# A decoder layer on one core: fp16 pairs, transposes by DMA, and a longer software pipeline

## What is computed

```
x = x + attention(layernorm(x))      # 8 heads of 128; q and k are RMS-normalised, turned (rotary),
                                     # causal softmax, products with wo
x = x + gelu(layernorm(x) @ ctx.T) @ ctx          # ctx: 375 rows of 256, one set per batch
x = x + ffn(layernorm(x))            # 256 -> 1024 -> 256, inputs, weights and biases
                                     # rounded to fixed point and clipped, relu between
```

## Time and profile before

| | |
|---|---|
| median of 3 runs | 731.43 us (731.16 to 732.57) |
| the profiled execution | 730.79 us |
| its span, first to last instruction | 729.1 us |
| PE, PEld busy | 697.2 us (96%), 609.9 us (84%) |
| DVE, ACT, POOL busy | 642.4 us (88%), 486.9 us (67%), 248.3 us (34%) |
| TensorE's granted clock, mean | 0.986 |
| DMA | 38.86 MB, 53 GB/s over the span |

### The profile page before, as it was taken

How to read it: one execution, slowest core, us unless ns; L and a number is a source line. 1 busy time by engine, 2 the same in 40 slices (tenths; PEclk the granted TensorE clock), 3 DMA queues, 4 the chain that set the end, 5 groups by cost and what they waited for, 6 DMA issues and landing times.

```text
span 729.1 us, 15114 instructions
## 1 busy us (share of the span) xinstructions
PE 697.2 (96%) x5504; PEld 609.9 (84%) x5504; DVE 642.4 (88%) x1232; ACT 486.9 (67%) x1226; POOL 248.3 (34%) x393
## 2 busy tenths in 40 slices
PE   5599999999999999999999999999999999999974
PEld 4488888888888888888888989889888888888863
DVE  6989999999999999999999999999999999998942
ACT  5667766677766677776667767666777766677742
POOL 1344333433332343333234243333334333433310
PEclk9899999999999999999999999999999999999996
DMA  8501110111111011111111111101111110111100
GB/s 268 204 8 49 49 48 24 54 57 49 55 48 42 26 55 55 48 52 51 32 35 55 55 48 48 52 22 47 55 53 50 48 47 24 54 50 43 49 7 13
DMA packets 23946, 38.86 MB, mean 53 GB/s; under 512 B 2048, under 2 KB 18896, under 8 KB 23664
## 3 DMA queue, kind: packets, MB, share of 16 engines
q1 hardware_dynamic: 23920, 38.51, 17.5%
HBM read 34.84 MB, written 3.67 MB: 53 GB/s over the span
## 4 chain that ended last, share of the span: by engine, by line
PE 89%; DVE 3%; ACT 3%; issue 2%; DMA 2%; SPq 0%; POOL 0%; POOLq 0%; DVEq 0%; ACTq 0%
PE psum L846 34%; PE psum L833 17%; PE psum L874 7%; PE psum L854 6%; PE psum L911 6%; PE psum L920 6%; PE psum L945 4%; PE psum L937 3%; PE psum L881 3%; PE psum L902 2%; DMA w_raw<-in_wv 1%; DMA w_raw<-in_w 1%; ACT qkn L743 1%; PE psum L927 1%; DVE turn_c L492 0%
## 5 line engine op out<-in xcount | busy, mean ns | idle before, releaser
L846 PE MATMUL psum<-wqkv_hi,xnT_hi 128*112 128x512 f32 x384 | 165.1, 430 | 4.8 <-DVE wqkv_lo L433 2.8
L846 PE MATMUL psum<-wqkv_lo,xnT_hi 128*112 128x512 f32 x384 | 152.3, 397 | 0.0
L846 PE MATMUL psum<-wqkv_hi,xnT_lo 128*112 128x512 f32 x384 | 131.4, 396 | 0.0
L697 ACT ACTIVATE sq<-psum 112x1024 f32<-112x1024 f32 x64 | 65.5, 1023 | 79.7 <-PE psum L846 79.7
L344 POOL TENSOR_TENSOR rstd<-ve,nhalf 112x1 f32<-112x1 f32 x96 | 55.4, 578 | 156.0 <-DVE ve L407 151.0
L351 POOL TENSOR_TENSOR rms<-ms,nhalf 112x8 f32<-112x8 f32 x64 | 106.3, 1662 | 5.0
L733 ACT ACTIVATE w_raw<-psum,rden 112x128 f32<-112x128 f32 x256 | 69.5, 384 | 45.7 <-DVE rden L519 45.7
L846 PEld LDWEIGHTS psum<-wqkv_hi,xnT_lo 128*112 128x112 f32 x384 | 67.5, 176 | 22.1
L846 PEld LDWEIGHTS psum<-wqkv_hi,xnT_hi 128*112 128x112 f32 x384 | 68.1, 177 | 21.4 <-issue 3.1
L476 DVE TENSOR_TENSOR turn_c<-psum,cos_t 112x1024 f32<-112x1024 f32 x64 | 78.1, 1220 | 6.2 <-ACT sq L697 5.6
L468 DVE TENSOR_REDUCE ss<-sq 112x4 f32<-112x512 f32 (+1 forms) x95 | 81.9, 862 | 0.0
(11 more groups left out here) (82 smaller groups left out, 1531.4 us busy)
## 6 DMA issues: line engine op xcount, KB each, us to landing
ctx_in<-in_ctx_rows SPq DMA_DIRECT2D x32, 375.0 KB
ctxT<-in_ctx_cols SPq DMA_DIRECT2D x32, 375.0 KB, 6.4
x_in<-in_x SPq DMA_DIRECT2D x32, 112.0 KB, 2.0
out_y<-y_out SPq DMA_DIRECT2D x32, 112.0 KB, 1.9
w_raw<-in_w SPq DMA_DIRECT2D x2, 1024.0 KB, 7.5
w_raw<-in_wq SPq DMA_DIRECT2D x2, 512.0 KB, 4.6
w_raw<-in_wk SPq DMA_DIRECT2D x2, 512.0 KB, 6.3
w_raw<-in_wv SPq DMA_DIRECT2D x2, 512.0 KB, 8.0
```

The source lines that it names most:

```text
L846: last = pe.matmul(ps[:, n, :], left[:, c, :], right[:, c, w, n * BANK:(n + 1) * BANK], start=c == 0 and left is xnT_hi and right is wqkv_ ...
```

## The change

It does eight things.

1. The weights wq, wk, wv, wo become fp16 pairs. Each is first scaled by a power of two: ScalarE squares it and sums along rows, TensorE sums over the partitions with a matrix of ones, VectorE bounds the sum, GpSimd takes the inverse root, VectorE keeps its exponent bits (`lift_weights`). The scales are taken back in the RMS constant for q and k, and in `residual_attention`, now a `scalar_tensor_tensor` with y_unit. Projections come in the order k, q, v.
2. xn and o become fp16 pairs, made before the transpose: ScalarE rounds (`round_xn`, `round_o`), VectorE subtracts (`split_xn`, `split_o`). So do q (`round_q0`, `round_q1` on ScalarE by head; `split_q` on VectorE by head, eight `scalar_tensor_tensor`) and k (`scale_k1`, `scale_k0` on ScalarE by head into kn, `round_k0`, `split_k`).
3. All 16-bit transposes, xn, q, k, o (both parts at once) and xq, are `dma_start_transpose` from SP's queue, SBUF to SBUF. Only xn2 (fp32) is still transposed on TensorE.
4. The keys' sum of cosine and sine part (`turn_k`) goes from VectorE to GpSimd.
5. `normalise_k` on VectorE is gone (see 2).
6. The PSUM banks are given out anew: q 3 and 4, k and scores 0 and 1, y 0, v 6 and 7, o 3 to 5, the FFN's hidden halves 5 and 6, ctx_out 7, and xn2T, h and the FFN's output 2.
7. p and o have buffers of their own; v's column of ones holds 16.
8. The loop is gone: 40 bodies are written out, each over up to nine batches a = i + 3 to i - 5, and the orders of all engines are new, with the waits that they need.

The core of the diff, new side first where a function is replaced as a whole:

```diff
+            def transpose_k(j):
+                sp.wait_ge(k_lo_done, done(j))
+                sp.dma_start_transpose(qkT[:, 1], qk16[:, 1].rearrange("t l n -> t (l n)")).then_inc(kT_landed, 16)
...
+            def transpose_x(j):
+                sp.wait_ge(xn_lo_done, done(j))
+                if j.has(1):
+                    sp.wait_ge(v1_ready, done(j.plus(-1)))
+                sp.dma_start_transpose(xT16[:, :, :], xn16[:, :, :].rearrange("t l n -> t (l n)")).then_inc(xT_landed, 16)
...
+            def turn_k(j):
+                pool.wait_ge(k_sin_done, done(j))
+                pool.tensor_tensor(turn_c[:, 1, :], turn_c[:, 1, :], turn_s[:, 1, :], ALU.add).then_inc(k_turned, 1)
...
+            def split_q(j):
+                dve.wait_ge(q_hi1_done, done(j))
+                for h in range(H):
+                    at = slice(h * D, (h + 1) * D)
+                    last = dve.scalar_tensor_tensor(out=qk16[:, 0, 1, at], in0=turn_c[:, 0, at], scalar=rms[:, 0, h:h + 1],
+                                                    in1=qk16[:, 0, 0, at], op0=ALU.mult, op1=ALU.subtract)
+                last.then_inc(q_lo_done, 1)
...
-                dve.tensor_tensor(heads(qkn[:, 1, :]), heads(turn_c[:, 1, :]),
-                                  rms[:, 1, :].unsqueeze(2).broadcast_to([T, H, D]), ALU.mult).then_inc(k_normed, 1)
...
+            def project_q(j):
+                if j.has(2):
+                    pe.wait_ge(o0_normed, done(j.plus(-2)))
+                if j.off == 1:
+                    pe.wait_ge(q_sin_done, done(j.plus(-1)))
+                project(0, 0, q_ps[:, 0, :], j)
+                project(0, 1, q_ps[:, 1, :], j).then_inc(q_ready, 1)
...
+                    hi, lo = xT16[:, c, :], xT16[:, MC + c, :]
+                    pe.matmul(dst, hi, wqkv[:, 0, c, w, cols], start=c == 0, stop=False)
+                    pe.matmul(dst, hi, wqkv[:, 1, c, w, cols], start=False, stop=False)
+                    last = pe.matmul(dst, lo, wqkv[:, 0, c, w, cols], start=False, stop=c == MC - 1)
```

More of the change, by code:

```diff
@@ L273, in x_at @@
[L273 to L281 removed]
+            sp.dma_start(x_in[:, 0, :], x[0:1].rearrange("o t m -> (o t) m")).then_inc(x_landed[0], 16)
@@ L321, in _ @@
+            for i in range(-3, B + 5):
+                body(i)
             for s in range(SLOTS):
@@ new lines, in round_projection, with prepare_projections @@
+            def round_projection(n):
+                for c in range(MC):
+                    act.wait_ge(w_lift_done, TURN.index(n) + 1)
+                    act.activation(wqkv[:, 0, c, n, :], w_raw[:, c, n, :], ACT.Copy, scale=w_lift[:, n:n + 1]).then_inc(w_hi_done, 1)
+            def prepare_projections():
+                one, two, three = TURN[0:3]
+                square_projection(one)
+                square_projection(two)
+                round_projection(one)
+                square_projection(three)
+                round_projection(two)
+                round_projection(three)
@@ new lines, in relu0 @@
+            def relu0(j):
+                if j.off >= B - 2:
+                    act.wait_ge(f0_ready, done(j))
+                if is_first(j):
+                    act.wait_ge(b_done, 2)
+                for c in range(0 * FC // 2, 1 * FC // 2):
+                    last = act.activation(f_int[:, c * T:(c + 1) * T], f0_ps[:, (c % (FC // 2)) * T:(c % (FC // 2) + 1) * T],
+                                          ACT.Relu, bias=b1_col[:, c:c + 1], scale=1.0 / W_FRAC)
+                last.then_inc(f0_int_done, 1)
@@ L897, in i_first, with sum_weights @@
-            def i_first(j):
-                return isinstance(j.base, int) and j.base + j.off == 0
-            def transpose_rows(dst, src, ready):
+            def sum_weights(n):
+                turn = TURN.index(n)
+                if turn == 0:
+                    pe.wait_ge(const_done, 6)
+                else:
+                    pe.wait_ge(w_sq_done, turn)
+                pe.wait_ge(w_squared, (turn + 1) * MC)
+                for c in range(MC):
+                    last = pe.matmul(w_sum_ps[:, n:n + 1], ones_pp[:, :], w_sum[:, n, c:c + 1], start=c == 0, stop=c == MC - 1)
+                last.then_inc(w_summed, 1)
@@ new lines, in project_out @@
+            def project_out(heads, j, first, last):
+                if is_first(j):
+                    pe.wait_ge(wo_done, 2)
+                for h in heads:
+                    pe.matmul(y_ps, oT16[:, h, :], wo16[:, 0, h, :], start=first and h == heads[0], stop=False)
+                    pe.matmul(y_ps, oT16[:, h, :], wo16[:, 1, h, :], start=False, stop=False)
+                    product = pe.matmul(y_ps, oT16[:, H + h, :], wo16[:, 0, h, :], start=False, stop=last and h == heads[-1])
+                return product
@@ new lines, in hidden_units0 @@
+            def hidden_units0(j):
+                if j.off == 28:
+                    pe.wait_ge(o0_normed, done(j.plus(3)))
+                if is_first(j):
+                    pe.wait_ge(w_q_done, 2)
+                for c in range(0 * FC // 2, 1 * FC // 2):
+                    for m in range(MC):
+                        last = pe.matmul(f0_ps[:, (c % (FC // 2)) * T:(c % (FC // 2) + 1) * T], w1T[:, m, c, :], xqT[:, m, :],
+                                         start=m == 0, stop=m == MC - 1)
+                last.then_inc(f0_ready, 1)
```

1267 lines of the change are left out of this document (633 added, 634 removed).

## The result

The changed kernel takes **654.65 us**, median of 4 runs (653.0 to 656.18), against 731.42 of the kernel before on the same chip: ratio 0.8947, 95% interval [0.8924, 0.8971]. The forecast was 657.0 (632 to 725). The profiled execution took 654.7 us, its span is 652.9 us, the mean granted clock 0.974.

The account below looks back on a forecast made before the run. TensorE bounded the kernel before, VectorE 9% behind; afterwards VectorE by a little, with an 18.5 us period. Fill 128 + 477 to the last keys + drain 48 + 2.8 = 656 span, time 657 us (632 to 725).

Parts of the forecast that it names:

- TensorE, 17.8 us: TensorE's work per batch: 21.4 less 2.4 for transposes moved off and 1.2 for fp16 pairs.
- VectorE, 18.1 us: VectorE's work per batch: 19.6 less 5.95 removed plus 4.5 added, making it the longest by a little.
- ScalarE, 16.8 us, and GpSimd, 10.5: Work per batch on these two engines: ScalarE 15.0 + 1.8, GpSimd 7.8 + 2.7; neither bounds.
- Stalls, 0.4 us: Waiting added per batch because TensorE and VectorE both need their whole period.
- slack of "about 1 us" at normalise_o: Room for normalise_o, between weigh_values and project_q two batches on, against 3.5 us of TensorE work.
- GpSimd, "I take 0": VectorE's slowdown beside GpSimd's keys' sum, taken as 0 as ordered; up to 1.8 us a batch kept for a rival.
- Rival B: GpSimd's sum slows VectorE, or normalise_o is late for project_q: period 20.3 us, 704 to 725 us; chance 0.22.
- DMA, 8.0 us a batch and 2.4 each: DMA engine time for all transposing transfers per batch, and for each of q, k or o; covered by their places.
- Rival C: Transposing DMAs bound: 18.8 + 3.7 = 22.5 us a batch, 761 to some 775 us; chance 0.17.
- The loop written out, 0: Instruction fetches for the written-out loop cost nothing, covered as long as they run ahead.
- TensorE's first wait on a DMA: Sign that would show the forecast wrong at once, as would a period above 20 us.
- Fill and drain, 128 and 48 us: Ends of the run: first output at about 128 us, not 74.3; last batch alone through the rest 48 us.

Follow-up runs that it names:

- e2: Changed kernel without the low fp16 parts of q for heads 4 to 7 (less VectorE work), in every batch but the first: 653.78 us.
- e9: Kernel before with only the pairs of wq, wk, wv and xn made fp16 (unscaled) in place of fp32r, transposes still on TensorE: 715.89 us.
- e3: Changed kernel without v's product of xn's low part with the weights' high part (less TensorE work), in every batch but the first: 654.17 us.
- e12: Changed kernel with two VectorE neighbours exchanged: xn's subtract and multiply ahead of the turn of q by the cosine: 691.30 us.
- e5: Changed kernel with k's 16-bit pair transposed by DMA once more per batch, into a tile nobody reads: 682.47 us.
- e14: Changed kernel with split_o later in VectorE's order and the second batch's xn made earlier, between wo's scale and split: 680.54 us.
- e6: Changed kernel with three more DMA transpositions of k's pair per batch, into spare tiles: 869.34 us.

## Why the prediction was right, step by step

- **TensorE, 17.8 us:** right in sum; e2, in which it alone is full, has 17.92. The 512-column product was put at 0.213 and is 0.216. The gain from the type was 0.9 of the 1.2 us for the projections; e9 shows 0.54, which is 36 x (0.231 - 0.216): the 0.2375 that I read for fp32r was drawn out by its late first product, the others are 0.23 apart (391.87, 392.10, 392.33). The rest of what TensorE lost, 3.47 - 0.54 = 2.9 us, is 0.2 more than the 2.7 that I gave it, so two errors in part cancel.
- **VectorE, 18.1 us:** right in sum, 17.9 by e3; "the longest by a little" was not to be told from TensorE. split_q was mis-sized: eight take 2.07 us (347.71 to 349.78), not 1.5, so 0.26 apart, not 0.19. Something else in the sum was 0.7 us too dear: 0.2 of it are the statistics (1.10 us in two places for 0.90 in one, where I added 0.4), the rest I did not trace. That the sum fits is in part luck.
- **ScalarE, 16.8 us, and GpSimd, 10.5:** 16.2 and 11.1 (90.46% and 61.88% of 17.94), hidden as forecast.
- **Stalls, 0.4 us:** there are next to none in the middle (TensorE waits 0.3 us in 100). The slack of "about 1 us" at normalise_o was right in place, wrong in kind: what is tight is the ring from turn_q over normalise_o to split_o, with 0.3 to 0.4 us. Together these put the period at 18.5 for 17.94, worth 14.6 us over 26 batches.
- **GpSimd, "I take 0":** right here, but for half of the named reason: the sum ends at 356.93, under reads of PSUM and a reduction, and the first instruction that it would hold starts at 356.98. But the price behind it was wrong. I read the earlier trace rows as 0.45 us per 0.72 of GpSimd for two SBUF operands; it is a hold until GpSimd is over (in the earlier trace rows add_b2 is over at 720.46 and quantise_x3 at 720.60), and a subtract and multiply of a single tile is held too (quantise_x3 is one). What kept the neighbours free was PSUM and the reduction, not "a single tile". e12 pays 1.35 us a batch for one exchange of neighbours. Rival B's mechanism exists; the order of this kernel steps past it by 0.05 us, which I had not worked out: that is luck.
- **DMA, 8.0 us a batch and 2.4 each:** (63.6% of 652.9 - 17.5% of 729.1) / 32 = 9.0, and 2.56. Rival C's 18.8 fell. The rooms were counted right (q: 7 us, measured 6.25), the tenants were not: SP's 2 us per issue was left out, though each queue that a step is moved to counts. e5 shows that there was no room for one issue more.
- **The loop written out, 0:** the instruction queues moved 0.84 MB in 0.5% of the span, and between 300 and 400 us the list of waits has none without a releaser. No kernel with the loop kept was run.
- **A sign that misled:** "TensorE's first wait on a DMA" was to show the forecast wrong at once. TensorE's longest wait is on one, 9.07 us for xn of the second batch at 37.91, but in the fill, and e14 shows it off the path; between 300 and 400 us it waits once for a transposition, 0.3 us.
- **Fill and drain, 128 and 48 us:** 135.4 and 52.4. 5 us of the first lie at one place: wo's scale, rounding and split were to end at 24.6, and the first turn started at 29.65, as split_wo alone waited 2.1 us for ScalarE. The early batches come 16.9 us apart (67.76, 84.69 in the chain), not 13.9 and 15.7. What makes the drain 4.4 us longer was not taken apart. This 12 us eats most of the 14.6 that the period gave: the total, 654.65 for 657, is by luck nearer to the forecast than its terms are.

## To carry to other kernels

When two engines are full, take work from both or leave it: here one alone gave nothing, and both together only as far as the next ring of waits allowed; add up that ring before trusting the second gain. Before work goes to GpSimd, list what VectorE runs beside it, and what waits for that: one plain SBUF-to-SBUF operation under a 2.4 us sum stood for the rest of the sum, and as it lay in a ring of waits in the kernel before, the same edit cost 47 us there and was worth 34 in the changed one. A DMA queue is an engine with an order of its own: price a transposition by the issuer's time and by the landing, not by the share of the DMA engines.

## What the runs showed of the hardware

- A VectorE instruction of 256 columns from one SBUF tile to another lasted 1.2 and 1.9 us beside a GpSimd sum, in place of 0.40, and was over 0.14 us behind it; a reduction and reads of PSUM did not stand. Beside GpSimd's root of eight columns the same kind of instruction took 0.41.
- A transposing transfer of 112 x 2048 fp16 between SBUF tiles: some 1.3 to 3.1 us to issue on SP, 4.0 to 6.5 us to landing, 1824 packets, 2.56 us of the 16 DMA engines.
- In e6, in which TensorE waits 4.7 us a batch at scores, the granted clock is 0.89 between 300 and 400 us, where the changed kernel has 1.00: this costs 2 us a batch beyond the wait itself.
- Products of 512 columns start 0.23 us apart in fp32r and 0.216 in fp16.
